# A fused delta-rule attention and ternary FFN on one core: half of the chunk inverses on GpSimd during the projection, the first two solve rounds in row halves

## The chip, the cores and the metric

The kernel runs on one core of a Trainium2 chip. The metric is the device time of one execution in microseconds. TensorE is PE here, VectorE DVE, ScalarE ACT, GpSimd POOL, and SyncE SP; SP and ACT issue the transfers.

## The reference

The input is x, 4 sequences of 2048 tokens with 256 channels, 4 heads of 64. In float32:

```
q, k, v = silu(conv4(x Wq)), silu(conv4(x Wk)), silu(conv4(x Wv));  beta = sigmoid(x Wb)
q, k normalised;  v = v * beta;  kb = k * beta
per head and chunk of 32 tokens:
    A = -(kb k^T) below the diagonal;  T = (I - A)^-1;  u = T v;  w = T kb
    attn = causal(q k^T);  u' = u - w S;  o = q S + attn u';  S = S + k^T u'
o = p0 fir3(v) + p1 fir15(v) + p2 fir63(v) + p3 o + p4 v     (p: softmax of gates, floored)
x = layernorm(x + rmsnorm(o) Wo)
x = layernorm(x + w3(gelu(h2(gelu(h1(silu(w1 x) * w2 x))))))
```

## The kernel before

It is four blocks with a barrier between them, each with hand-written queues per engine. Tokens go in 16 steps of 128 tokens of all 4 sequences, so a step holds 16 streams (4 sequences x 4 heads), `NS`.

**`project`.** For a step, PE makes six blocks (`cb` 0 to 5: two each of q, k and v) of projections (L224), ACT and DVE convolve them in `acc` (L334, L379), and ACT applies silu into `yT` (L307). Work of the step before is laid in between: `keys` turns k to tokens (`ktok`, L314) and forms the products k k^T of all 16 streams in `side`, copied to `kfull` (L324); `small` makes gates and the sums of q squared from `sq` (POOL, L424); `values` turns v to `vtok` (L395). The squared norm of k is the diagonal of k k^T: POOL picks it (`picked`, L434, four operations of 32 partitions), DVE sums it (`kk`, L398), and then POOL zeroes the 32x32 diagonal blocks and all left of them in `kfull` (L439). SP stores four pieces of the diagonal blocks as `a_s` (L176), and the rest as `kk_s` (L184), and loads `xt` of the step after next (L161). Twice in the block and once after it, `blocks_in` reads the diagonal blocks back into `tri`, whose partition is step and stream and whose 8 slots are 4 chunks x 2 groups of eight steps (L103).

**`weights_fir`.** DVE makes the mixing weights and the scales; `gamT` and `neg_gamT` are beta over the norm of k. Then come 64 rounds `n`. In a round PE convolves 4 channels with Toeplitz matrices (`conv`, L613), DVE multiplies with the weights (`prods`, L725), and POOL adds three parts in two operations (`two` L783, `mixed` L787). In rounds 0 to 59 DVE also does one operation of the forward substitution that inverts all 8 slots of `tri` in place: for column j an outer product (`outer`, L743) in an even round and the `update` (L747) in the odd one, 8j(31-j) elements each. The rows are scaled in two goes (L750), ACT turns the inverses (`turned_inv`, L641), and SP stores both as `d_s` and `t_s` (L566). SP loads the Toeplitz matrices in three pieces of 256-byte rows for each pair of rounds (L555), and the windows `win` of the next head (L548), the last of them when the head before has had its last round but two.

**`delta`.** The inverse of a 128-token block is built from the four 32x32 inverses by rounds of products: N = L x diag, A = N x diag^T, B and C repeated products, with partial copies by ACT (`nmat`, `r1`, `r2`, L1161) and sums by DVE in `tt` (L1244, L1246, L1261). They are made for step t+1 during step t. PE's order in a step is: state product, N, T (transposes), Q (q k^T), solve (L1063), W (output projection), outputs, A, B, C. ACT's is: N, T, the two `us`, `osq` once DVE has added `mix` to `o` (L1194), then A and B. DVE's is: Q, W, outputs, the sum over `osq` (L1290), statistics, terms A and B, C, then the right side and the norm. `N` needs banks that DVE's evacuation of the last C has freed.

**`ffn`** runs on PE with weights in two halves.

## Time and profile before

| | |
|---|---|
| three runs | 2434.59, 2437.59, 2437.62 us, median 2437.59 |
| the profiled execution | 2435.2 us, its span 2433.3 us |
| share of the span | PE 89%, DVE 51%, ACT 37%, POOL 24% |
| mean granted clock of TensorE | 0.956 |
| projection, weights and FIR, delta, FFN | 360.5, 251.8, 486.2, 1334.8 us |

The share of PE is a mean over four stages with different limits, and the chain that ended last, followed back, lies in the FFN alone. So the first three stages have to be read by their timelines. A row of a timeline has start, length, engine, line, operation and tiles, and in brackets how long the engine had been idle and what ended that. A float32 product is two records of PE.

### The profile page before, as it was taken

How to read it: one execution, taken by the hardware profiler on the slowest of the kernel's cores; microseconds unless marked ns; L12 is line 12 of the kernel's file. 1: busy time of each engine (PE TensorE's matmuls, PEld its weight loads, DVE VectorE, ACT ScalarE, POOL GpSimd, SP SyncE). 2: the span in 40 equal slices, each digit the busy share in tenths (PEclk: the TensorE clock that was granted, in tenths of full speed). 3: DMA queues.
4: the chain of work that ended last, by engine and by line, in shares of the span. 5: the costliest groups of instructions: out<-in, count | busy, mean ns of one | idle time of the engine just before them, and what ended most of it. 6: DMA issues, size and time to landing. Idle time of an engine off the chain costs nothing.

```text
span 2433.3 us, 40589 instructions
## 1 busy us (share of the span) xinstructions
PE 2157.0 (89%) x15412; PEld 1855.9 (76%) x15412; DVE 1235.5 (51%) x1872; ACT 895.2 (37%) x1425; POOL 593.4 (24%) x416
## 2 busy tenths in 40 slices
PE   7887865655699999967999999999999999999998
PEld 6776754555588888855888888888888888888887
DVE  5776758896477777762323332333333333323332
ACT  4554530002233334313434443444344334433442
POOL 2555555896344444430000000000000000000000
PEclk9999987887799999987999999999999999999999
DMA  3558759787989989925000000000000000000000
GB/s 131 194 197 204 194 200 211 198 207 236 241 229 249 250 235 241 254 79 219 1 18 17 0 17 17 17 0 17 17 17 0 17 17 17 0 17 17 18 1 18
DMA packets 346603, 257.53 MB, mean 106 GB/s; under 512 B 281394, under 2 KB 315698, under 8 KB 336434
## 3 DMA queue, kind: packets, MB, share of 16 engines
q1 hardware_dynamic: 333682, 232.65, 35.1%
q10 hardware_dynamic: 12864, 24.12, 2.8%
q8 instruction: 36, 0.59, 0.1%
q14 instruction: 21, 0.17, 0.0%
HBM read 156.85 MB, written 99.88 MB: 106 GB/s over the span
## 4 chain that ended last, share of the span: by engine, by line
PE 52%; issue 1%; DVE 1%; ACT 0%; DMA 0%; SPq 0%; POOL 0%; DVEq 0%; ACTq 0%; POOLq 0%
PE B L1611 46%; PE O L1639 5%; PE T L1567 1%; DVE yb L1738 0%; ACT gate L1677 0%; DMA wr<-wr_s 0%; SPq L1500 0%; DVE stats L1769 0%; ACT L1677 0%; DVE z L1764 0%; DVE z L1760 0%; DVE z L1783 0%; POOL rstd L1819 0%; SPq L1514 0%; DVEq L1733 0%
## 5 line engine op out<-in xcount | busy, mean ns | idle before, releaser
L1611 PE MATMUL B<-act1l,wr 128*128 128x512 f32 x1024 | 398.4, 389 | 0.0
L1611 PE MATMUL B<-act1h,wr 128*128 128x512 f32 x1024 | 398.3, 389 | 0.0
L1611 PE MATMUL B<-act0h,wr 128*128 128x512 f32 x1024 | 398.3, 389 | 0.0
L1611 PE MATMUL B<-act0l,wr 128*128 128x512 f32 x1024 | 398.3, 389 | 0.0
L1691 ACT ACTIVATE yb<-B,scol 128x512 f32<-128x512 f32 x256 | 176.2, 688 | 581.0 <-PE B L1611 581.0
L1726 DVE TENSOR_TENSOR act0l<-yb,act0h 128x512 fp32r<-128x512 f32 x256 | 176.1, 688 | 377.9 <-ACT act0h L1694 375.7
L1816 POOL TENSOR_TENSOR rstd<-mv,ln_eps 128x4 f32<-128x4 f32 x16 | 3.2, 199 | 1309.2 <-DVE mv L1777 1309.2
L379 DVE SCALAR_TENSOR_TENSOR acc<-proj,taps,acc 128x512 f32<-128x512 f32 x288 | 214.4, 750 | 92.3 <-ACT acc L334 83.7
L1726 DVE TENSOR_TENSOR act1l<-yb,act1h 128x512 fp32r<-128x512 f32 x128 | 88.6, 692 | 295.5 <-ACT act1h L1694 295.5
L224 PE MATMUL proj<-xt,w_qkv 128*128 128x262 f32 x768 | 195.0, 400 | 35.9 <-DMA xt<-in_xt 19.4
L1611 PEld LDWEIGHTS B<-act1h,wr 128*128 128x128 f32 x1024 | 192.2, 188 | 39.9
L1611 PEld LDWEIGHTS B<-act0h,wr 128*128 128x128 f32 x1024 | 192.2, 188 | 39.9
L1611 PEld LDWEIGHTS B<-act0l,wr 128*128 128x128 f32 x1024 | 192.2, 188 | 39.9
L1611 PEld LDWEIGHTS B<-act1l,wr 128*128 128x128 f32 x1024 | 192.2, 188 | 39.9
L1611 PE MATMUL B<-xh,wr 128*128 128x512 f32 x512 | 202.7, 396 | 11.8 <-DMA wr<-wr_s 7.6
L613 PE MATMUL conv<-toe,win 128*128 128x192 f32 x512 | 139.2, 433 | 83.1 <-DMA win<-v_s 41.8
L1611 PE MATMUL B<-xl,wr 128*128 128x512 f32 x512 | 200.8, 392 | 0.0
L613 PEld LDWEIGHTS conv<-toe,win 128*128 128x128 f32 x512 | 127.8, 316 | 94.4 <-DMA win<-v_s 43.0
L224 PEld LDWEIGHTS proj<-xt,w_qkv 128*128 128x128 f32 x768 | 141.5, 192 | 72.2 <-DVE acc L379 28.6
L1738 DVE SCALAR_TENSOR_TENSOR yb<-B,scol,gate 128x512 f32<-128x512 f32 x128 | 94.8, 750 | 183.7 <-ACT gate L1677 128.1
L783 POOL TENSOR_TENSOR two<-prods 128x256 f32<-128x256 f32 x64 | 123.6, 1932 | 17.7 <-DVE prods L725 17.7
L1611 PEld LDWEIGHTS B<-xh,wr 128*128 128x128 f32 x512 | 97.0, 189 | 37.7 <-DVE yb L1738 10.1
(164 smaller groups left out, 3477.6 us busy)
## 6 DMA issues: line engine op xcount, KB each, us to landing
qk_s<-yT SPq DMA_DIRECT2D x16, 1024.0 KB, 5.8
kk_s<-kfull SPq DMA_DIRECT2D x16, 1024.0 KB, 3.9
qk<-qk_s SPq DMA_DIRECT2D x16, 1024.0 KB, 6.7
lt<-kk_s SPq DMA_DIRECT2D x15, 1024.0 KB, 5.3
wraw<-in_ffn_w ACTq DMA_DIRECT2D x16, 704.0 KB, 6.4
wr_s<-wround ACTq DMA_DIRECT2D x16, 704.0 KB, 9.5
toe<-in_firp SPq DMA_DIRECT2D x64, 160.0 KB, 3.6
xt<-in_xt SPq DMA_DIRECT2D x16, 524.0 KB, 4.0
```

What stands on the lines that cost most here:

```text
L224: last = nc.tensor.matmul(proj[cb % 2][:, 2 * half:2 * half + 2, 0:XW], w_qkv[:, k, cb * P:cb * P + P], xt[p][:, k, 2 * half:2 * half + 2, ...
L379: nc.vector.scalar_tensor_tensor(out=acc[cb % 3][:, :, :], in0=proj[cb % 2][:, :, j:j + P], scalar=taps[:, cb, j:j + 1], in1=acc[cb % 3][: ...
L613: last = nc.tensor.matmul(conv[n % 2][:, c // 2, c % 2 * NF * WIN:(c % 2 + 1) * NF * WIN], win[h % 2][:, :, g * FCH + c], toe[part % 2][:, ...
L783: nc.gpsimd.tensor_tensor(two[n % 2][:, :, :], part[:, 0, :, :], part[:, 1, :, :], ALU.add).then_inc(two_done, 1)
L1567: last = nc.tensor.transpose(T[:, k, b * P:b * P + P], x1[p][:, b, k * P:k * P + P], ident)
L1611: last = nc.tensor.matmul(B[slot % 4][:, :], w, part, start=(k == 0 and i == 0), stop=(k == kts - 1 and i == len(parts) - 1))
L1639: last = nc.tensor.matmul(O[:, b, :], sets[0][i][:, k, b * P:b * P + P], wr[:, W3 + k * D:W3 + k * D + D], start=(k == 0 and i == 0), stop ...
L1691: last = nc.scalar.activation(dst, B[slot % 4][:, :], ACT.Gelu, scale=scol[:, slot:slot + 1])
L1726: nc.vector.tensor_tensor(sets[s][1][:, m, :], yb[n % 3][:, :], sets[s][0][:, m, :].bitcast(f32), ALU.subtract).then_inc(lo_done, 1)
L1738: nc.vector.scalar_tensor_tensor(out=dst, in0=B[(2 * m + 1) % 4][:, :], scalar=scol[:, HT + m:HT + m + 1], in1=gate[m % 2][:, :], op0=ALU. ...
L1816: nc.gpsimd.tensor_tensor(rstd[:, :], mv[:, :, 1:2].rearrange("p b o -> p (b o)"), ln_eps[:, :], ALU.add).then_inc(rs_link, 1)
```

## The change

In the projection, the norms of k come from `ktok` squared by POOL (`sqk`) and summed by DVE, so that `picked`, the mask, and `a_s` go; `kfull` is stored whole, and each step reads its own diagonal blocks back into `tri`. After step 8 the scales of the first eight steps are made, and POOL runs the substitution of their 4 slots, columns 1 to 24, between the squares of steps 10 to 16; the rest of the columns and the row scaling come first on POOL in the next block. There DVE does the other 4 slots, both operations of a column in one round, in rounds 0 to 29. The Toeplitz matrices come ready from DRAM in one transfer (0.79 MB) per pair of rounds. `d_s` and `t_s` are stored by halves at the pairs 2, 4, 18 and 20. In the delta stage, N and A are made in two products per stream, of 64 output rows each, over the columns that are filled; ACT copies the filled blocks in three (N) or two (A) pieces; and ACT's copies of A stand ahead of `osq`. The loops of the projection are partly written out. The diff, cut to its core:

```diff
-BLOCK_PARTS = ((0, STEPS // 2), (STEPS // 2, 3 * STEPS // 4), (3 * STEPS // 4, STEPS))
+NSUB = GRP // P
+EARLY_STEPS = STEPS // NSUB
+EARLY_COLS = {10: (1, 5), 11: (5, 9), 12: (9, 12), 13: (12, 15), 14: (15, 18), 15: (18, 21), 16: (21, 25)}
+EARLY_END = 25
...
-def blocks_in(queue, io, keep, part):
-    first, end = BLOCK_PARTS[part]
-    g, rows = first // (STEPS // 2), slice(first * NS % P, (end * NS - 1) % P + 1)
+def blocks_in(queue, io, keep, t):
+    first = t * NS % P
     for q in range(NQ):
-        queue.dma_start(keep["tri"][rows, q * (GRP // P) + g, :, :],
-                        io["a_s"][q * CH:q * CH + CH, first * NS:end * NS, :].rearrange("i n j -> n i j")
-                        ).then_inc(keep["tri_in"], 16)
+        queue.dma_start(keep["tri"][first:first + NS, q * NSUB + t // EARLY_STEPS, :, :],
+                        io["kk_s"][q * CH:q * CH + CH, t * NS:t * NS + NS, q * CH:q * CH + CH].rearrange("i n j -> n i j")
+                        ).then_inc(keep["tri_in"][t // EARLY_STEPS], 16)
...
+class Substitution:
+    def __init__(self, engine, keep, half, outer):
+        self.engine, self.slots = engine, slice(half, SLOTS, NSUB)
+        self.tri, self.outer = keep["tri"][:, self.slots, :, :], outer
+        self.gamT, self.neg_gamT = keep["gamT"][:, self.slots, :], keep["neg_gamT"][:, self.slots, :]
+    def scaled_columns(self):
+        for r in range(0, CH, 8):
+            g = self.neg_gamT[:, :, 0:r + 8]
+            g = bass.AP(tensor=g.tensor, offset=g.offset, ap=[g.ap[0], g.ap[1], [0, 8], g.ap[2]])
+            last = self.engine.tensor_tensor(self.tri[:, :, r:r + 8, 0:r + 8], self.tri[:, :, r:r + 8, 0:r + 8], g, ALU.mult)
+        return last
+    def products(self, j):
+        return self.outer[:, 0:SLOTS // NSUB * (CH - 1 - j) * j].rearrange("p (s i c) -> p s i c", s=SLOTS // NSUB, c=j)
+    def outer_product(self, j):
+        row = self.tri[:, :, j, 0:j]
+        row = bass.AP(tensor=row.tensor, offset=row.offset, ap=[row.ap[0], row.ap[1], [0, CH - 1 - j], row.ap[2]])
+        return self.engine.tensor_tensor(self.products(j), bcast(self.tri[:, :, j + 1:CH, j], j), row, ALU.mult)
+    def update(self, j):
+        below = self.tri[:, :, j + 1:CH, 0:j]
+        return self.engine.tensor_tensor(below, below, self.products(j), ALU.add)
+    def scaled_rows(self):
+        return self.engine.tensor_tensor(self.tri, self.tri, bcast(self.gamT, CH), ALU.mult)
+    def zero_above(self):
+        for i in range(CH - 1):
+            last = self.engine.memset(self.tri[:, :, i, i + 1:CH], 0.0)
+        return last
+    def ones_on_diagonal(self):
+        return self.engine.memset(self.tri.rearrange("p s i j -> p s (i j)")[:, :, 0:CH * CH:CH + 1], 1.0)
...
-                    for q in range(NQ):
-                        rows = slice(q * CH, q * CH + CH)
-                        sp.dma_start(io["a_s"][rows, bass.ds(t * NS, NS), :], kfull[p][rows, :, rows]).then_inc(diag_stored[p], 16)
+                    sp.dma_start(io["kk_s"][:, t * NS:t * NS + NS, :], kfull[p][:, :, :]).then_inc(kk_stored[p], 16)
                     sp.wait_ge(ktok_out, n)
                     sp.dma_start(row(io["k_s"], t), ktok[p][:, :, :]).then_inc(k_stored[p], 16)
                     sp.wait_ge(vtok_out, n + 1)
-                    sp.dma_start(io["v_s"][:, :, bass.ds(t + 1, 1), :, :].rearrange("h p o b d -> p h (o b d)"),
+                    sp.dma_start(io["v_s"][:, :, t + 1:t + 2, :, :].rearrange("h p o b d -> p h (o b d)"),
                                  vtok[p][:, :, :, :].rearrange("p h b d -> p h (b d)")).then_inc(v_stored[p], 16)
-                    sp.wait_ge(kk_masked, n)
-                    sp.dma_start(io["kk_s"][:, bass.ds(t * NS, NS), :], kfull[p][:, :, :]).then_inc(kk_stored[p], 16)
+                    sp.wait_ge(kk_stored[p], 16 * (t // 2 + 2))
+                    blocks_in(sp, io, keep, t)
...
+                    early = isinstance(t, int) and t == EARLY_STEPS + 1
+                    if early:
+                        pe.wait_ge(gam0_done, 1)
+                        nc.tensor.transpose(gam_ps, gam0[:, :, :, :].rearrange("p t r s -> p (t r s)"), ident).then_inc(gam0_turned, 1)
                     turn(lambda hh, b: yT[p][:, KT + hh, b * P:b * P + P]).then_inc(ktok_ready, 1)
+                    if early:
+                        pe.wait_ge(gam0_out, 2)
...
+                    if isinstance(t, int) and t == EARLY_STEPS + 1:
+                        act.wait_ge(gam0_turned, 1)
+                        for scale, dst in ((-1.0, keep["neg_gamT"]), (1.0, keep["gamT"])):
+                            nc.scalar.activation(dst[:, 0:SLOTS:NSUB, :], gam_ps.rearrange("p (q i) -> p q i", i=CH),
+                                                 ACT.Copy, scale=scale).then_inc(gam0_out, 1)
...
+                    act.wait_ge(sqk_done, t + 1)
                     nc.scalar.activation(ktok[p][:, :, :], tok[:, :, :], ACT.Copy).then_inc(ktok_out, 1)
                     act.wait_ge(kk_stored[p], n * 16 + 16)
-                    act.wait_ge(kk_summed, t + 1)
...
+                nc.scalar.activation(ebeta[:, :, :], raw[:, 0:NE, NGATE:NGATE + HEADS], ACT.Exp, scale=-1.0).then_inc(exp0_done, 1)
...
-                    dve.wait_ge(diag_picked, t * NQ + NQ)
                     nc.vector.tensor_copy(vtok[p][:, :, :, :].rearrange("p h b d -> p b h d"),
                                           tok[:, :, :].rearrange("p b (h d) -> p b h d", d=DK)).then_inc(vtok_out, 1)
-                    nc.vector.tensor_reduce(kk[:, bass.ds(t, 1), :, :].rearrange("p o r s -> p (o r s)"), picked[p][:, :, :],
-                                            AX.X, ALU.add).then_inc(kk_summed, 1)
+                    dve.wait_ge(sqk_done, t + 3)
+                    nc.vector.tensor_reduce(kk[:, bass.ds(t, 1), :].rearrange("p o h -> p (o h)"),
+                                            sqk[:, :, :].rearrange("p b (h d) -> p (b h) d", d=DK), AX.X, ALU.add).then_inc(kk_summed, 1)
+                def first_scales():
+                    def link(ins, n):
+                        ins.then_inc(gam0_link, 1)
+                        dve.wait_ge(gam0_link, n)
+                    dve.wait_ge(kk_summed, EARLY_STEPS + 2)
+                    nc.vector.tensor_scalar(ssk0[:, :, :].rearrange("p (t b) h -> p t (b h)", b=BATCH), kk[:, 0:EARLY_STEPS, :],
+                                            L2_EPS, None, ALU.add)
+                    dve.wait_ge(exp0_done, 1)
+                    link(nc.vector.tensor_scalar(ebeta[:, :, :], ebeta[:, :, :], 1.0, None, ALU.add), 1)
+                    link(nc.vector.tensor_tensor(half0[:, :, :], ssk0[:, :, :], ebeta[:, :, :], ALU.mult), 2)
+                    link(nc.vector.reciprocal(half0[:, :, :], half0[:, :, :]), 3)
+                    for par in range(2):
+                        last = nc.vector.tensor_copy(gam0[:, :, par, :],
+                                                     half0[:, :, :].rearrange("p (t b) (k r) -> p t r (b k)", t=EARLY_STEPS, r=2)[:, :, par, :])
+                    last.then_inc(gam0_done, 1)
...
-                def diagonals(t, p, n):
-                    for q in range(NQ):
-                        rows = slice(q * CH, q * CH + CH)
-                        if q:
-                            pool.wait_ge(diag_picked, t * NQ + q)
-                        nc.gpsimd.tensor_tensor(picked[p][rows, :, :], kfull[p][rows, :, rows],
-                                                bcast_mid(const[rows, C_ONE:C_ONE + CH], NS), ALU.mult).then_inc(diag_picked, 1)
-                    pool.wait_ge(diag_stored[p], n * (16 * NQ) + 16 * NQ)
-                    pool.wait_ge(diag_picked, t * NQ + NQ)
-                    nc.gpsimd.tensor_tensor(kfull[p][:, :, :], kfull[p][:, :, :], bcast_mid(const[:, C_OFF:C_OFF + P], NS),
-                                            ALU.mult).then_inc(kk_masked, 1)
...
+                def key_squares(t, p):
+                    pool.wait_ge(ktok_out, t + 1)
+                    pool.wait_ge(kk_summed, t + 2)
+                    nc.gpsimd.tensor_tensor(sqk[:, :, :], ktok[p][:, :, :], ktok[p][:, :, :], ALU.mult).then_inc(sqk_done, 1)
...
+                for t in range(STEPS + 1):
+                    if t < STEPS:
+                        squares(t, t % 2)
+                    if t:
+                        key_squares(t - 1, 1 - t % 2)
+                    if t == EARLY_STEPS + 1:
+                        pool.wait_ge(keep["tri_in"][0], 16 * NQ * EARLY_STEPS)
+                        sub.zero_above().then_inc(keep["sub_link"], 1)
+                    if t in EARLY_COLS:
+                        first, end = EARLY_COLS[t]
+                        if first == 1:
+                            pool.wait_ge(gam0_out, 2)
+                            pool.wait_ge(keep["sub_link"], 1)
+                            sub.scaled_columns().then_inc(keep["sub_link"], 1)
+                            pool.wait_ge(keep["sub_link"], 2)
+                            sub.ones_on_diagonal()
+                        early_columns(nc, pool, sub, keep, first, end)
+def early_columns(nc, pool, sub, keep, first, end):
+    for j in range(first, end):
+        pool.wait_ge(keep["sub_link"], 2 * j)
+        sub.outer_product(j).then_inc(keep["sub_link"], 1)
+        pool.wait_ge(keep["sub_link"], 2 * j + 1)
+        sub.update(j).then_inc(keep["sub_link"], 1)
...
-                    for f, k in enumerate(FIRS):
-                        src = io["firp"]
-                        sp.dma_start(toe[n % 2][FIRST[f]:, :, f, :],
-                                     bass.AP(tensor=src.tensor, offset=(n * TCH * NF + f) * FIRPAD + FIRST[f],
-                                             ap=[[1, P - FIRST[f]], [NF * FIRPAD, TCH], [1, WIN]])).then_inc(toe_in[n % 2], 16)
+                    sp.dma_start(toe[n % 2][:, :, :, :], io["toe"][n]).then_inc(toe_in[n % 2], 16)
...
+                    if n in D_OUT:
+                        sp.wait_ge(inv_done[D_OUT[n]], 1)
+                        blocks_out("d_s", tri, D_OUT[n])
+                    if n in T_OUT:
+                        sp.wait_ge(turned[T_OUT[n]], 1)
+                        blocks_out("t_s", turned_inv, T_OUT[n])
...
-                    j = n // 2 + 1
-                    if j <= COLS:
-                        link(outer_product(j) if n % 2 == 0 else update(j))
-                    if n + 1 == ROWS_EARLY or n + 1 == 2 * COLS:
-                        if n + 1 == ROWS_EARLY:
-                            dve.wait_ge(upper_zero, 1)
-                        rows = slice(0, EARLY) if n + 1 == ROWS_EARLY else slice(EARLY, CH)
-                        scaled_rows(rows).then_inc(inv_done, 1)
+                    if n < COLS:
+                        link(sub.outer_product(n + 1))
+                        link(sub.update(n + 1))
+                    if n == COLS:
+                        dve.wait_ge(upper_zero, 1)
+                        sub.scaled_rows().then_inc(inv_done[1], 1)
...
+                late = Substitution(nc.gpsimd, keep, 1, None)
+                pool.wait_ge(tri_in[1], 16 * NQ * EARLY_STEPS)
+                late.zero_above().then_inc(above_zero, 1)
+                sub = Substitution(nc.gpsimd, keep, 0, keep["outer0"])
+                early_columns(nc, pool, sub, keep, EARLY_END, CH - 1)
+                pool.wait_ge(keep["sub_link"], 2 * (CH - 1))
+                sub.scaled_rows().then_inc(inv_done[0], 1)
                 pool.wait_ge(columns_scaled, 1)
-                for i in range(CH - 1):
-                    nc.gpsimd.memset(tri[:, :, i, i + 1:CH], 0.0)
-                last = nc.gpsimd.memset(tri[:, :, :, :].rearrange("p s i j -> p s (i j)")[:, :, 0:CH * CH:CH + 1], 1.0)
-                last.then_inc(upper_zero, 1)
+                late.ones_on_diagonal().then_inc(upper_zero, 1)
...
+        FILLED = {"N": ((slice(0, P // 2), slice(0, CH)), (slice(P // 2, P), slice(0, 3 * CH))),
+                  "A": ((slice(0, P // 2), slice(CH, P)), (slice(P // 2, P), slice(3 * CH, P)))}
...
-                        elif kind in "NABC":
+                        elif kind in "NA":
+                            for j in range(4):
+                                c = par * BH + half * 4 + j
+                                for out, cols in FILLED[kind]:
+                                    left = (lt if kind == "N" else nmat)[:, c, out]
+                                    right = (ddiag[p] if kind == "N" else tdiag[p])[:, c, cols]
+                                    last = nc.tensor.matmul(bank[out, j, cols], left, right, start=True, stop=True)
+                        elif kind in "BC":
...
-                        rows, cols = REGION.get(kind, (slice(0, P), slice(0, P - CH if kind == "N" else P)))
-                        if kind == "T":
-                            dst = oT[:, g, :].rearrange("p (b n) -> p b n", b=BATCH)
-                        else:
-                            dst = {"N": nmat, "A": r1, "B": r2}[kind][rows, c, cols]
+                        if kind == "N":
+                            for rows, cols in BELOW:
+                                last = nc.scalar.activation(nmat[rows, c, cols], bank[rows, :, cols], ACT.Copy)
+                            last.then_inc(act_out, 1)
+                            continue
+                        if kind == "A":
+                            for rows, cols in ABOVE:
+                                last = nc.scalar.activation(r1[rows, c, cols], bank[rows, :, cols], ACT.Copy)
+                            last.then_inc(act_out, 1)
+                            continue
+                        rows, cols = REGION.get(kind, (slice(0, P), slice(0, P)))
+                        dst = oT[:, g, :].rearrange("p (b n) -> p b n", b=BATCH) if kind == "T" else r2[rows, c, cols]
...
+                    if pre:
+                        copy_rounds("A", seq, round0)
                     act.wait_ge(mixed, t + 1)
                     nc.scalar.activation(osq[:, :, :, :], o[:, :, :, :], ACT.Square).then_inc(sq_done, 1)
                     if pre:
-                        copy_rounds("A", seq, round0)
```

## Rows read from the trace of the kernel before

**Rows 1.** Busy time by stage: stretch, length, engines, PEclk, DMA share, GB/s
```profile
0.00:360.50 360.50, 291.72 (x2560) 236.73 (x2560) 246.24 (x352) 168.56 (x275) 184.75 (x101) 0.96 0.63 188
360.50:612.30 251.80, 141.47 (x562) 129.61 (x562) 201.66 (x151) 21.96 (x14) 184.01 (x163) 0.78 0.81 213
612.30:1098.50 486.20, 418.11 (x6018) 391.06 (x6018) 333.53 (x617) 168.44 (x321) 205.21 (x119) 0.95 0.85 221
```

**Rows 2.** Waits of the projection: us in total, times, longest
```profile
PE proj L224 <- DMA xt<-in_xt: 19.4, 3, 9.0
```

**Rows 3.** Timeline of SP's queue in the projection
```profile
191.66 13.07 SPq L103 DMA_DIRECT2D tri<-a_s  x4
```

**Rows 4.** Timeline of ACT in the projection, the copies of `ktok`
```profile
191.69 1.01 ACT L314 ACTIVATE ktok<-tok 128x1024 f32<-128x1024 f32 x1
...
219.41 1.02 ACT L314 ACTIVATE ktok<-tok 128x1024 f32<-128x1024 f32 x1 [0.28 <-PE tok L233]
...
340.82 1.02 ACT L314 ACTIVATE ktok<-tok 128x1024 f32<-128x1024 f32 x1 [0.23 <-ACT yT L307]
```

**Rows 5.** Timeline of DVE in the projection
```profile
316.90 0.68 DVE L398 TENSOR_REDUCE kk<-picked 128x512 f32 x1
```

**Rows 6.** Groups by form in the projection: busy us, mean ns, idle before
```profile
L439 POOL TENSOR_TENSOR kfull<-kfull,const 128x2048 f32<-128x2048 f32 x16 | 72.6, 4535 | 14.2 <-DMA a_s<-kfull 12.9
...
L424 POOL TENSOR_TENSOR sq<-yT 128x1024 f32<-128x1024 f32 x16 | 30.3, 1893 | 145.7 <-PE side L273 128.1 <-ACT yT L307 17.7
```

**Rows 7.** Groups by line, 362 to 600 us
```profile
L783 POOL TENSOR_TENSOR two<-prods 128x256 f32<-128x256 f32 x64 | 123.6, 1932 | 17.7 <-DVE prods L725 17.7
...
L747 DVE TENSOR_TENSOR tri<-tri,outer 128x240 f32<-128x240 f32 (+14 forms) x30 | 56.2, 1872 | 0.0
```

**Rows 8.** Timeline of the rounds
```profile
395.15 0.96 DVE L725 TENSOR_TENSOR prods<-conv,pwT 128x768 f32<-128x768 f32 x1 [1.96 <-ACT pwT L659]
...
486.40 0.96 DVE L725 TENSOR_TENSOR prods<-conv,pwT 128x768 f32<-128x768 f32 x1
...
494.28 6.70 PE L613 MATMUL conv<-toe,win 128*128 128x192 f32 x24 [8.13 <-DMA win<-v_s]
...
561.14 8.62 PE L613 MATMUL conv<-toe,win 128*128 128x192 f32 x32 [1.38 <-DMA toe<-in_firp]
...
583.48 0.40 DVE L743 TENSOR_TENSOR outer<-tri 128x240 f32<-128x240 f32 x1
```

**Rows 9.** The stage's end: timeline, and the busy times of ten us
```profile
596.37 0.73 POOL L787 TENSOR_TENSOR mixed<-two,prods 128x256 f32<-128x256 f32 x1
...
598.27 1.46 SPq L562 DMA_DIRECT2D mix_s<-mixed  x1
...
600.00:610.00 10.00, 0.00 (x0) 0.00 (x0) 0.00 (x0) 0.00 (x0) 0.00 (x0) 0.50 1.02 423
```

**Rows 10.** Timeline of one step of the delta stage
```profile
826.64 2.96 PE L1032 MATMUL R<-tdiag,nmat 128*96 128x96 f32 x32
...
829.45 1.06 ACT L1194 ACTIVATE osq<-o 128x1024 f32<-128x1024 f32 x1 [9.67 <-DVE o L1286]
...
830.41 3.08 ACT L1161 ACTIVATE r<-R 96x384 f32<-96x384 f32 x8
830.54 1.22 DVE L1290 TENSOR_REDUCE ss<-osq 128x16 f32<-128x1024 f32 x1 [1.12 <-ACT osq L1194]
...
831.02 3.18 PE L1032 MATMUL R<-r,nmat 128*64 128x64 f32 x64 [1.43 <-ACT r L1161]
...
836.62 3.81 PE L1032 MATMUL R<-ddiag,lt 128*128 128x96 f32 x32 [0.36 <-DVE tt L1261]
```

**Rows 11.** The same stage: timeline of two solves; group by form of ACT's copies
```profile
815.90 2.08 PE L1063 MATMUL Y<-x,tt 128*64 128x64 f32 x64
...
843.22 2.08 PE L1063 MATMUL Y<-x,tt 128*64 128x64 f32 x64
...
L1161 ACT ACTIVATE nmat<-R 128x384 f32<-128x384 f32 x52 | 25.5, 491 | 56.4 <-PE R L1032 56.4
```

191 lines of the change are left out of this document (78 added, 113 removed).

## The prediction

> **What bounds the kernel now.** I read the busy times by stage first [rows 1]. The program is four blocks in a row: projection (0 to 360.5 us), weights and FIR (to 612.3), delta rule (to 1098.5), FFN. The FFN is not touched, so only the first three can move; the chain that ended last starts inside the FFN and says nothing of them. For those I went through the timelines and asked which wait closes each loop.
>
> *Projection.* No engine is full. One step takes 20.2 us (six from 219.4 to 340.8 [rows 4]), and DVE's convolution of block 5, ACT's copies and PE's products close a circle. The exception is one step: `tri<-a_s` holds SP's queue 13.07 us [rows 3], so the next `xt` is late (three waits of PE for `xt`, the first load's among them, make 19.4 us [rows 2]), and 27.7 us lie between two `ktok` copies instead of 20.2: 7.5 us lost.
>
> *Weights and FIR.* In 64 rounds PE convolves, DVE weighs and does one substitution product, GpSimd adds twice. DVE and GpSimd take turns: `two` averages 1.93 us [rows 7], and the addition of the same size without DVE beside it 0.73 [rows 9]. At each new head PE stops for `win` (8.13 us) [rows 8].
>
> *Delta.* A step is 27.3 us, from solve to solve [rows 11]. PE is busy through most of it, but what lets the next step begin is DVE: it idles until ACT's `osq` is done, then works without a gap for 6.1 us, and round N starts behind the evacuation of round C [rows 10].
>
> **The change, part by part.** Each is a difference against the profiled 2435.2 us (span 2433.3), 2.4 us under the median 2437.6, which I carry over unchanged.
>
> *Projection, removed.* The bulk reads of `a_s` become four 64 KB reads per step, as many issues as the `a_s` stores that go; SP's wait for `kk_stored` ends before `vtok` is stored, hence free. The lost 7.5 us return: **-7.5**. If the four small reads hold SP like the large ones, this is 0.
>
> *Projection, DVE.* The sum over `picked` (512 elements, 0.68 us [rows 5]) becomes one over `sqk` (1024 elements). The delta stage's sum of that shape takes 1.22 us [rows 10]. The wait for `picked` that goes is about 0.25. On the circle, +0.3 in some 14 steps: **+4.2**. `first_scales` waits once for ACT's Exp, with a table load there and one back, and does six small operations on DVE; `keys` of step 9 waits for one transpose and two copies; no row prices them, I take **+3.7** together (0 to 8).
>
> *Projection, GpSimd.* `picked` and the mask (4.5 us a step) leave, `key_squares` comes (1.9, as `sq` [rows 6]). Of the substitution, column j has two operations of 4j(31-j) elements. At 2.2 ns an element (2048 in 4.54 us [rows 6]) the fullest step, columns 21 to 24 (6080 elements), costs 13.4 us, the other full ones 11 to 12.6. With 3.8 us of squares, 16.4 lie under the 20.2 of a step, so PE's wait for `sq` stays covered; at over 2.8 ns an element it would not be. Behind the last `ktok` copy (341.8 [rows 4]) GpSimd needs 1.9 + 13.4 us: 357 to 358. SP's last store, `kk_s` behind the mask, goes out with the copies of `kfull` and no longer ends the block: **-2.2** (to +2).
>
> *Second stage, start.* Loop start now 34.6 us behind the stage's (395.15 [rows 8]). The late read of `tri`, the `toe` memsets and two thirds of the Toeplitz issues go. But GpSimd first does 31 memsets (4 us), columns 25 to 30 (4480 elements, 9.9) and the scaled rows (4096 elements, 9.0), taking turns with DVE's softmax work. I put the start at 32: **-2.5** (-8 to +4).
>
> *Rounds 0 to 29.* Half the slots, but both operations of a column in one round: by round 30 DVE has multiplied and added 39,680 elements, exactly what it has done by then today, in 60 operations instead of 30. An operation of 240 elements takes 0.40 us [rows 8], 30 of them with 39,680 elements 56.2 us [rows 7], which is 1.04 ns an element and 0.5 each, of which about 0.15 is its own and 0.35 GpSimd's turn. Thirty more cost 4 to 15; I take 8. The head's stall at round 16 (8 us for PE, some 6 for DVE, which has rounds in hand) falls under DVE's longer rounds, the two early 2 MB stores (`d_s`, `t_s`) delay a Toeplitz load by some 3: **+5** (-1 to +15).
>
> *Rounds 30 to 63.* Today 110.7 us (486.40 [rows 8] to 597.1 [rows 9]), with DVE's operation in nearly all. After it: scaled rows 4.4, then only the weighing (0.96) and GpSimd's two additions (1.5) against PE's 2.15 a round (8.62 for four [rows 8]): 33 rounds are 71 us. Per two rounds the queues move 0.79 MB of `toe` and, for one head, 0.52 of `win`, with `mix_s` 1.57 MB; at 263 GB/s (213 at a share of 0.81 [rows 1]) that is 6.0 us, at the 423 of the stretch with only large stores [rows 9] 3.7, against PE's 4.3; large rows prevail, so I lean to the second, and the late stores 4 MB more: 8 us of waiting. Two head changes, one half hidden: 8. Sum 91.5: **-19** (-32 to -5).
>
> *Its end.* The last `mix_s` store (issued at 598.3 [rows 9], the stage ending at 612.3) stands behind 4 MB of `t_s` and more of `d_s` and takes 12 us to land; alone, about 5: **-6.5**. Stage: **-23**.
>
> *Delta, round N.* Per slot one product of 128x128 by 96 columns (119 ns a record [rows 10]) becomes two with 64 rows, 32 and 96 columns wide, each two records. Round pairs on alternating halves take 32.5 ns a record (2.08/64 [rows 11]); B and C, not alternating, average 50 [rows 10]. So halves overlap, and the 96-column half sets the time, at round A's 92 ns: 16x2x92 = 2.9 us instead of 3.8. ACT now copies in three pieces (128, 256 and 128 elements; 0.49 us for 384 [rows 11] and 1.06 for 1024 [rows 10] make 0.26 and 0.38, pipelined about 0.79) instead of 0.49, so it paces the round, and Q waits for its banks. Gain 0.3 a step (from 0.4 to a loss of 0.3).
>
> The Trainium skill ("TensorE: Matmul & The Clock Gate", section "The mechanism") says that a weight load overlaps running matmuls only when the row group differs, which it does not here. By that N and A would each be some 4.2 us. The alternating records above speak against it.
>
> *Delta, round A.* It already has 96 columns, so its 2.96 us stay. ACT's copies now come before `osq`: the last A bank is ready 3.15 us after A's start, its two copies end at 3.8, `osq` at 4.9. Today `osq` ends at 3.9 [rows 10]. PE's 1.43 us wait for the first copy of A goes, but PE isn't what closes the step: DVE's sum waits for `osq`, and behind it stand statistics, both terms, C's evacuation and so N. Loss 1.0 a step (0.65 to 1.75). Net +0.7 in 14 steps: **+10**.
>
> Sum: -1.8 - 23 + 10 = **-15 us**, 2437.6 - 15 = 2423.
>
> **The rivals.** *Forecast, with its own range 2408 to 2433:* chance 0.50.
>
> *Halves do not overlap* (slower). The two products of a slot run one after the other: (40 + 92)x2x16 ns = 4.2 us for N and A, 40 being what is left for C's records in the 3.18 us that B and C take. A's last copy then ends near 5.1, `osq` at 6.1, 2.2 late, and N loses 0.4: +2.6 a step, +36. With -23 and -2 from the other stages, 2449. It decides from about 1.8 us a step. For it: such unequal halves aren't in the trace. Against: rows 11. Chance 0.12.
>
> *GpSimd's turns cost more* (no change, or slower). If a column's second operation waits for a whole addition and the start waits for the 9 us scaled rows, rounds 0 to 29 cost +15 and the start +4; with the transfers nearer 263 GB/s in the second half the stage gains only 10. 2437.6 - 2 - 10 + 10 = 2436, up to 2443. For it: `two` at 1.93. Chance 0.20.
>
> *The second half runs at PE's pace, the delta stage is even.* No queue waits in rounds 31 to 63, SP's stall gone, the copies packed: 2437.6 - 35 - 4 + 3 = 2402. For it: the single contiguous `toe` transfer in place of three of 256-byte rows. Against: `win` still arrives late at each head. Chance 0.16.
>
> *The early inverses don't hide.* GpSimd above 2.8 ns an element, each step 10 to 16 drawn out by 2 to 3 us: +15, near 2438. Against: 2.2 is measured beside the same DVE work. Chance 0.02.
>
> **How the numbers follow.** This kernel's runs tell 0.2%, 4.9 us, from no change. The forecast's range lies mostly beyond it: 0.46 faster, 0.04 same; the fast case 0.16 faster; the costly turns 0.04 faster, 0.08 same, 0.08 slower; no overlap 0.12 slower; the last 0.02 same. So 0.66 faster, 0.14 same, 0.20 slower. The range of 8 in 10 runs from inside the fast case to between the two slow ones: 2400 to 2446.
>
> **What the profile would show.** Right: no wait of PE for `xt` but the first; `ktok` copies about 20.5 us apart; GpSimd's 960-element operations near 2.1 us, `sq` never awaited; in the second stage rounds of 3.1 us, then of 2.2; delta steps of 28.0 us with DVE's wait for `osq` near 2.1 instead of 1.1; N near 2.9. Wrong: N at or over 3.8 and A over 3.5 (no overlap); rounds above 2.6 us after the thirtieth (transfers); a delta step under 27.3, which would mean DVE's stretch does not close the circle and the 0.7 has the wrong sign.

## The result and the profile after

| | us, median | runs | ratio to before, 95% interval |
|---|---|---|---|
| before | 2436.1 | 2431.0 to 2437.6 | |
| after | 2483.9 | 2479.5 to 2486.9 | 1.0199 (1.0176 to 1.0221) |

The change makes the kernel 2.0% slower, some 48 us. Forecast was 2423. The profiled execution has a span of 2485.1 us, against 2433.3 before.

The busy times by stage of the kernel after, in the columns of [rows 1]:

```profile
0.00:359.90 359.90, 293.65 (x2561) 237.78 (x2561) 255.40 (x358) 171.62 (x279) 146.22 (x121) 0.97 0.61 179
359.90:598.20 238.30, 139.16 (x561) 129.91 (x561) 158.11 (x149) 21.13 (x12) 151.78 (x174) 0.79 0.74 247
598.20:1149.00 550.80, 431.02 (x7042) 399.74 (x7042) 347.51 (x618) 217.74 (x513) 192.41 (x119) 0.89 0.72 197
```

The first stage is even (359.9 instead of 360.5), the second 13.5 us shorter, and the third 64.6 us longer. In the third, TensorE's granted clock has fallen from 0.95 to 0.89 and PE has 1024 more records, yet only 13 us more busy time. So it waits. Who for, by the waits of PE there (us in total, times, longest):

```profile
PE R L1071 <- DMA tdiag<-t_s: 47.3, 8, 15.6
PE X L1101 <- issue: 30.5, 6, 5.3
PE R L1082 <- ACT r L1219: 12.5, 15, 0.8
PE R L1057 <- ACT nmat L1209: 8.8, 12, 0.9
```

The second row is new. "issue" is time in which PE waited for nothing that the profile shows, and it stands ahead of X, the products from the state that open a step, 4.7 to 5.3 us in every second step: at each of the six branches back of PE's loop, which makes seven turns of two steps. The first row, PE's wait for `tdiag`, is longer than before too: there it is 36.5 us in three waits, here 3.4 to 4.3 us of it stand in six of the steps without a stop. PE's timeline around one of the stops, to be held against [rows 10]:

```profile
...
835.68 2.81 PE L1071 MATMUL R<-tdiag,nmat 128*64 128x96 f32 x64
838.32 2.16 PE L1082 MATMUL R<-r,nmat 128*64 128x64 f32 x32
841.32 1.22 PE L1082 MATMUL R<-r,nmat 128*32 128x32 f32 x32 [0.83 <-ACT r L1219]
847.86 3.75 PE L1101 MATMUL X<-S,qk 128*128 128x128 f32 x16 [5.32 <-issue]
851.54 3.85 PE L1071 MATMUL R<-ddiag,lt 128*64 128x32 f32 x64
...
```

After the stop, X takes 3.75 us instead of 2.05, and N 3.85 instead of 2.86: the granted clock was 0.54 over the 5 us of the stop and 0.50 over the next 3.5 us, the 1.2 GHz level. The page's list of DMA queues (packets, MB, share) says what else has grown; before it was 36 packets and 0.59 MB:

```profile
q8 instruction: 97, 1.59, 0.3%
```

What was forecast of the third stage is there too. In a turn's good step (start at 805.68) `osq` comes 4.03 us behind A instead of 2.81, DVE's sum waits for it 2.24 us instead of 1.12, and ACT copies N's slots in threes, of which PE's Q waits 0.9 for the last:

```profile
805.68 2.81 PE L1071 MATMUL R<-tdiag,nmat 128*64 128x96 f32 x64
...
809.71 1.06 ACT L1254 ACTIVATE osq<-o 128x1024 f32<-128x1024 f32 x1
...
810.80 1.22 DVE L1351 TENSOR_REDUCE ss<-osq 128x16 f32<-128x1024 f32 x1 [2.24 <-ACT osq L1254]
...
818.04 2.86 PE L1071 MATMUL R<-ddiag,lt 128*64 128x32 f32 x64 [3.48 <-DMA tdiag<-t_s]
...
822.84 2.27 PE L1057 MATMUL R<-qk 64*128 64x128 f32 x32 [0.92 <-ACT nmat L1209]
```

A step here is 30.0 us, against 27.3 before [rows 11], and 34.2 with the stop in it; over eleven steps the mean is 32.5.

The second stage, from the waits of PE after its rounds have begun, and PE and SP where the longest one falls:

```profile
PE conv L678 <- DMA toe<-in_toe: 30.1, 12, 8.2
PE conv L678 <- DMA win<-v_s: 22.9, 3, 8.5
```
```profile
514.72 8.81 PE L678 MATMUL conv<-toe,win 128*128 128x192 f32 x32 [1.36 <-DMA toe<-in_toe]
531.75 8.63 PE L678 MATMUL conv<-toe,win 128*128 128x192 f32 x32 [8.22 <-DMA toe<-in_toe]
```
```profile
515.54 0.60 SPq L636 DMA_DIRECT2D d_s<-tri  x1
...
519.59 0.33 SPq L627 DMA_DIRECT2D toe<-in_toe  x1
...
524.44 0.59 SPq L636 DMA_DIRECT2D t_s<-turned_inv  x1
536.89 0.33 SPq L627 DMA_DIRECT2D toe<-in_toe  x1
```

### The profile page after: what moved, and what is told of

Same layout as the page of the kernel before. It is cut to its first block, busy times and chain, and to the rows that moved or that the text cites. A ratio compares the mean times of both kernels' runs of the same rounds, so it can differ in the third digit from the quotient of the medians.

```text
span 2485.1 us, 42333 instructions
## 1 busy us (share of the span) xinstructions
PE 2169.3 (87%) x16436; PEld 1865.8 (75%) x16436; DVE 1215.1 (49%) x1877; ACT 946.8 (38%) x1620; POOL 509.8 (21%) x447
## 3 DMA queue, kind: packets, MB, share of 16 engines
q8 instruction: 97, 1.59, 0.3%
## 4 chain that ended last, share of the span: by engine, by line
PE 51%; issue 1%; DVE 1%; ACT 0%; DMA 0%; SPq 0%; POOL 0%; DVEq 0%; ACTq 0%; POOLq 0%
PE B L1672 45%; PE O L1700 5%; PE T L1628 1%; DVE yb L1799 0%; ACT gate L1738 0%; DMA wr<-wr_s 0%; SPq L1561 0%; DVE stats L1830 0%; ACT L1738 0%; DVE z L1825 0%; DVE z L1821 0%; DVE z L1844 0%; POOL rstd L1880 0%; SPq L1575 0%; DVEq L1794 0%
## 5 line engine op out<-in xcount | busy, mean ns | idle before, releaser
L259 PE MATMUL proj<-xt,w_qkv 128*128 128x262 f32 x768 | 196.6, 403 | 29.3 <-DVE acc L439 20.2
L678 PE MATMUL conv<-toe,win 128*128 128x192 f32 x512 | 137.1, 432 | 80.1 <-DMA win<-v_s 32.5
L1209 ACT ACTIVATE nmat<-R 32x128 f32<-32x128 f32 (+1 forms) x192 | 58.6, 305 | 228.4 <-PE R L1071 226.1
```

The source lines that it names most:

```text
L259: last = nc.tensor.matmul(proj[cb % 2][:, 2 * half:2 * half + 2, 0:XW], w_qkv[:, k, cb * P:cb * P + P], xt[p][:, k, 2 * half:2 * half + 2, ...
L678: last = nc.tensor.matmul(conv[n % 2][:, c // 2, c % 2 * NF * WIN:(c % 2 + 1) * NF * WIN], win[h % 2][:, :, g * FCH + c], toe[part % 2][:, ...
L1209: last = nc.scalar.activation(nmat[rows, c, cols], bank[rows, :, cols], ACT.Copy)
```

## The experiments

All figures are medians, with the interval of the ratio to the kernel before, timed beside it on the same chip. The kernel before itself had medians of 2434.1 to 2437.3 there, so a difference between kernels that were timed on different chips is good to some 3 us. A step's length is the mean over eleven steps, from SP's loads of `lt`.

### Which stage

**e1_delta_of_before**: the function `delta` of the kernel before in the kernel after. `kk_s` comes unmasked there, and this `delta` does not clear what lies above the diagonal, so the mask is left out of the computation. 

> The kernel after the change, but the third stage (delta) is the one of the kernel before, with its 384-element copies, full-width products of rounds N and A and osq ahead of the A copies. The trace of after puts the loss in the third stage (550.8 us instead of 486.2) and a gain of 14 us in the first two. If that reading holds (theory T), this kernel takes 2436 - 14 = 2422, range 2416 to 2428, and its third stage 486 +- 4. Rival: part of the loss is carried over from the first two stages (later stores of the inverses, another layout of the program), then it stays above 2440.

Measured 2421.0, 0.9937 (0.9920 to 0.9954), a step 27.33. **e2_only_delta**: the function `delta` of the kernel after in the kernel before. 

> The kernel before, with the third stage (delta) of the kernel after alone. Theory T (the stages add up): 2436 + 62 = 2498, range 2490 to 2506, with waits of PE called issue ahead of the products from the state (X) in every second step and the queue 8 of instructions at some 95 packets. Rival: the third stage of after only loses because its inverses or buffers come in another way from the new stages, then 2436 to 2450.

Measured 2478.5, 1.0165 (1.0146 to 1.0184), a step 30.67, 65 packets in queue 8. So the first two stages give 16 us and the third takes it back four times over. It takes 63 us with the new stages ahead of it (2483.9 less 2421.0) but only 41 with the old ones, which I had not expected: something in `delta` depends on what stands ahead of it. One difference is in the trace. Of the six branches back, in e2 only every second one has a stop (5.3 to 5.9 us); the other three have 0.2 us.

```profile
729.88 2.02 PE L1064 MATMUL X<-S,qk 128*128 128x128 f32 x16 [0.22 <-issue]
...
793.74 3.76 PE L1064 MATMUL X<-S,qk 128*128 128x128 f32 x16 [5.62 <-issue]
```

### Which part of the third stage

**e3_full_products** and **e4_unrolled** start from the kernel after:

```diff
e3:
-for out, cols in FILLED[kind]:
-    left = (lt if kind == "N" else nmat)[:, c, out]
+rows_out, cols_out = (slice(0, P), slice(0, P - CH)) if kind == "N" else REGION["A"]
+left = (lt if kind == "N" else nmat)[:, c, rows_out]
e4:
-with pe.Fori(0, MID // 2) as i:
+for i in range(MID // 2):
```

> The kernel after; rounds N and A of the third stage are made again by one product of full width for each slot (16 fewer instructions a round), while ScalarE keeps its copies by filled blocks and its order (A copies ahead of osq). Theory 1 (the longer loop of TensorE is what costs: its instructions are fetched again in every turn): queue 8 back to some 36 packets, no waits called issue ahead of X, granted clock of the third stage back to 0.94, time 2422 + 10 = 2432, range 2424 to 2442. Theory 2 (ScalarE's order and its three copies cost): the loss stays, 2465 to 2485, with the waits called issue gone or not.

> The kernel after, with TensorE's loop over the steps of the third stage written out, so that no branch goes back; the products and waits are the same. Theory 1 as a miss at the branch back: more packets in queue 8 than after's 97 (about 120), but the waits of 5.3 us ahead of X are gone or under 1 us, time 2440 to 2455. Theory 1 as a bandwidth of fetching: as after or worse, 2475 to 2500, with waits called issue spread over other lines. Theory 2 (ScalarE's order and copies): 2475 to 2485 with the waits gone.

Measured 2466.1, 1.0121 (1.0104 to 1.0138), and 2461.7, 1.0107 (1.0090 to 1.0124). Each takes away the stop ahead of X (0.2 to 0.4 us are left of it in e3, nothing in e4), and each only about 20 of the 63 us: e4 lies above the 2440 to 2455 that theory 1 gave it. Theory 1 alone falls. With full products and 41 packets a step is still 30.87: 3.5 us over e1's, and this is ScalarE's share.

**e5_order_alone** and **e6_copies_alone** put ScalarE's two edits singly into the kernel before, **e7_products_alone** the halving:

```diff
e5  +copy_rounds("A", seq, round0)
     act.wait_ge(mixed, t + 1); osq
e5  -copy_rounds("A", seq, round0)
e6  +N copied by BELOW (three pieces a group), A by ABOVE (two)
e7  +N: rows 0:64 and 64:128 over columns 0:96;  A: rows 0:64 and 64:96 over columns 32:128
```

> The kernel before, with one part of the third stage alone: ScalarE's copies of round A stand ahead of osq. The run with full products showed the next round N starting 11.3 us after round A instead of 10.0, because tt comes later. Order theory: 1.3 us a step over 14 steps, 2437 + 18 = 2455, range 2449 to 2461. Rival (ScalarE's pieces do all of it, the order alone is harmless because B's products no longer wait 1.4 for r): 2437 +- 5.

> The kernel before, with one part of the third stage alone: ScalarE copies round N's slots in three pieces and round A's in two (nmat is cleared once). Copies theory: one group of N takes 0.95 us instead of 0.49, so Q starts about 1.8 us later behind N: 14 x 1.9 = 27, 2437 + 27 = 2464, range 2452 to 2472. Rival (the order does it all, copies lie beside the products): 2437 +- 5.

> The kernel before, with one part of the third stage alone: rounds N and A are made in row halves, over all the columns that the old copies read, so twice the instructions of TensorE for the same elements. Fetching theory (the loop of two steps no longer stays loaded): queue 8 at some 65 packets or more, a wait called issue in every turn, 2437 + 20 = 2457, range 2445 to 2465. Rival 1 (the halves overlap and take back a part, no fetching): 2437 - 10 to 2437. Rival 2 (halves do not overlap): 14 x 5.8 = 2437 + 80.

Measured 2458.9, 1.0104 (1.0082 to 1.0126); 2460.2, 1.0106 (1.0089 to 1.0123); 2521.2, 1.0344 (1.0302 to 1.0386). Order and pieces cost 22 and 24 us, and together, e3 less e1, 45: they add up. In e5 N waits 2.1 to 2.5 us for `tt` in every step (0.36 before [rows 10]), and sometimes that costs a second time: of thirteen such rounds two took 6.8 us, five 5.4 and the others 3.8. N's row and the window over it (PE, PEld, DVE, ACT, POOL busy, clock, DMA share, GB/s), with the clock at 0.53, for an N of 6.81 us instead of 3.81:

```profile
815.98 6.81 PE L1032 MATMUL R<-ddiag,lt 128*128 128x96 f32 x32 [2.51 <-DVE tt L1275]
```
```profile
816.00:822.70 6.70, 6.70 (x33) 6.70 (x34) 4.14 (x10) 1.47 (x3) 1.90 (x2) 0.53 1.07 357
```

In e6 the pieces act at two places, N and, unforeseen, A. Eight copies of 64 rows and fewer take 3.11 us where four of 96x384 took half that, B's copies and with them C come later, and B and C take 4.14 us instead of 3.18 [rows 10]:

```profile
810.03 3.11 ACT L1175 ACTIVATE r<-R 64x384 f32<-64x384 f32 x8
...
810.92 4.14 PE L1043 MATMUL R<-r,nmat 128*64 128x64 f32 x64 [1.71 <-ACT r L1175]
```

e7 is no clean test of the halving, since I cut A into 64 and 32 rows: A took 9.49 us instead of 2.96, while N, in 64 and 64 rows, took 2.86 instead of 3.81.

```profile
810.83 2.86 PE L1034 MATMUL R<-ddiag,lt 128*64 128x96 f32 x64
...
827.27 9.49 PE L1034 MATMUL R<-tdiag,nmat 128*64 128x96 f32 x64
```

These two do not add up to its 85 us. Its undisturbed step is 31.2 us instead of 27.3, which is 3.9 for the 6.5 and -0.95, and four of its branches back have the stop:

```profile
PE X L1064 <- issue: 28.2, 4, 7.9
```

A step with the stop is some 8.7 us longer: 14 x 3.9 + 4 x 8.7 = 89, 85 measured. So a good third of e7 is the stops too, with 74 packets in queue 8.

**e8_order_undone**: the kernel after with the old order. 

> The kernel after, with osq ahead of the A copies again, as before. Order theory: 2484 - 18 = 2466, range 2458 to 2474. Rival (order harmless): 2484 +- 5.

Measured 2501.2, 1.0271 (1.0254 to 1.0289). A miss of the other sign: 17 us slower than after. Its undisturbed step is 29.7 us, 0.3 shorter, but its stops ahead of X are longer, 7.7 to 8.7 us instead of 4.7 to 5.3. What the order costs alone it does not cost beside the stops; why the stop grows was not tried.

**e9_pieces_for_N** keeps of the new `delta` only N's pieces; **e10_half_N_added** adds N's row halves to it:

```diff
e9, in delta of the kernel after, with the products of e3 and the order of before:
-for rows, cols in ABOVE:
-    last = nc.scalar.activation(r1[rows, c, cols], bank[rows, :, cols], ACT.Copy)
+nc.scalar.activation(r1[rows, c, cols], bank[rows, :, cols], ACT.Copy)      (rows, cols of REGION["A"])
e10, for N alone:
+for out, cols in FILLED["N"]:
+    last = nc.tensor.matmul(bank[out, j, cols], lt[:, c, out], ddiag[p][:, c, cols], start=True, stop=True)
```

> The kernel after, its third stage changed back to full-width products in N and A, one copy of 384 elements a group for A, and osq ahead of the A copies; only N's copies stay in three pieces. If the parts add up, the pieces of N alone cost 0.4 to 0.6 us a step (Q starts 5.0 instead of 4.6 behind N, as in the run with the copies alone) and the pieces of A the rest of that run's 1.6: 2421 + 7 = 2428, range 2423 to 2434. Rival (N's pieces are the costly ones): 2440 or more.

> The kernel of the run before, with round N alone in row halves over its filled columns (16 more products a step, half of what the change adds). Fetching theory with a limit by length: queue 8 at 60 to 97 packets, a wait called issue of 3 to 6 us in every turn of the two-step loop, 2428 + 20 = 2448, range 2438 to 2460. If the loop of this length still stays loaded: 36 to 41 packets, no such wait, N 1 us shorter but Q still behind the copies: 2420 to 2428.

Measured 2428.5, 0.9975 (0.9964 to 0.9987), and 2480.0, 1.0186 (1.0169 to 1.0203). So N's pieces cost 7.5 us over e1 (9 by the ratios), and by difference A's pieces, which were not run alone, cost the other 16 of e6. And sixteen more products a step bring the whole of the stops back, for 51 us where I had said 20, although N itself is 0.9 us shorter:

```profile
809.95 2.05 PE L1108 MATMUL X<-S,qk 128*128 128x128 f32 x16
812.44 2.86 PE L1078 MATMUL R<-ddiag,lt 128*64 128x32 f32 x64 [0.44 <-DVE tt L1326]
...
834.59 3.18 PE L1089 MATMUL R<-r,nmat 128*64 128x64 f32 x64 [1.43 <-ACT r L1224]
844.09 3.75 PE L1108 MATMUL X<-S,qk 128*128 128x128 f32 x16 [6.32 <-issue]
```

### What the stops are

**e11_before_unrolled**, **e13_padded_by_16** and **e14_padded_by_8** are the kernel before with more code and its own work; **e16_half_N_unrolled** is e10 with the loop written out.

```diff
e13, e14, behind the waits of from_state:
+for _ in range(16):      (8 in e14)
+    nc.tensor.matmul(X[0][0:1, 0, 0, 0:1], qk[p][:, KT, 0:1], S[:, 0, 0, 0:1], start=True, stop=True)
```

> The kernel before, with TensorE's loop over the steps of the third stage written out: the same products and waits, only more code, each fetched once. Fetching theory: some 75 packets in queue 8 instead of 36, waits called issue of some 3 us a step as in the written-out kernel after, 2437 + 25 = 2462, range 2450 to 2485. Rival (fetching is free as long as no branch goes back, and the waits in the written-out kernel after came from its late inverses): 2437 +- 5.

> The kernel before, with 16 products of one element each added to every step of TensorE's loop, behind the waits of the products from the state (they write a bank that is overwritten next). The work stays that of before, the loop grows by as many instructions as half of round N's halves add. If the length of the loop alone brings the fetching: queue 8 near 92 packets, a wait called issue of some 6 us in every turn, 2437 + 50 = 2487, range 2465 to 2500. Rival (the fetching needs the denser rows of instructions of the halved rounds): 36 packets, 16 x 0.03 to 0.06 us a step, 2437 to 2450.

> As the run before with 8 such products a step. If the loop's limit lies between the loop of before (which stays loaded) and that plus 16: either 36 packets and 2437 to 2443, or near 92 packets and 2465 to 2500; nothing between, for the loop either stays or is fetched whole. I take the second, 0.6: the written-out loop took 3 packets of 16 KB a step, so two steps are 6, and partly filled ones at both ends make it 7 or 8.

> The kernel with pieces for N and halves in N alone, with TensorE's loop over the steps written out. If only the branch back costs: no wait called issue ahead of X, 2428 - 2 = 2426, range 2420 to 2432. If the halved round is too dense for the fetching (the written-out kernel after waited 3.5 us a step ahead of N): 2440 to 2460, with that wait again.

Measured 2438.2, 1.0009 (0.9999 to 1.0020), 72 packets; 2439.9, 1.0015 (1.0005 to 1.0024), 37 packets; 2449.0, 1.0051 (1.0035 to 1.0068), 91 packets; 2430.5, 0.9968 (0.9956 to 0.9979), 81 packets. Written out, the code is fetched in passing and costs nothing that can be told; so it is the branch back that costs. But length does not decide: with 16 products more nothing is fetched again, with 8 more something is. The step of e14 is 27.4 us all the same, and its time falls between the two cases of which I had said that nothing lies between. Its stops lie elsewhere, in the loop of the FFN, whose code nobody had touched:

```profile
PE B L1613 <- issue: 10.5, 6, 2.1
```

That pointed to where a loop lies. I counted TensorE's instructions of 64 bytes in the compiled programs, in blocks of 16 KB (a packet of queue 8 is 1.59 MB / 97 = 16 KB). The counts are in no profile:

```
            delta's loop        FFN's loop         packets   PE waits for issue
before      14.02 to 20.21  7   37.44 to 43.80  7     36     none
e13         14.27 to 20.96  7   38.44 to 44.80  7     37     none
e14         14.15 to 20.58  7   37.94 to 44.30  8     91     in FFN
e9          19.15 to 25.33  7   42.57 to 48.93  7     41     none
e10         19.65 to 26.33  8   43.57 to 49.93  7     96     in delta
after       20.15 to 27.33  8   44.57 to 50.93  7     97     in delta
e2          15.02 to 22.21  8   39.44 to 45.80  7     65     in delta
```

The number behind a stretch is how many blocks it touches; waits of 0.5 us and less are left out. The loops are 6.19 blocks long before, 6.69 with 16 products more a step, 7.19 with 32. The packets bear the lengths out: written out, the six further turns bring 36 packets more than before in e11 (6.0 a turn) and 40 more than e9 in e16 (6.7 a turn). Where a loop starts, only the count says. A shift of 0.1 block is in all of these; I chose it, and from 0.08 to 0.13 the table comes out as runs show: a loop that touches seven blocks stays loaded, one that touches eight is fetched again. e10, after and the FFN of e14 have six stops each, with 54 to 56 packets more than where the loop stays (e10 less e17, after less e9, e14 less before), some nine for each stop. e2 has three, and e7, whose loop has as many products as e2's, has four, with 29 and 38 packets more than before, nine or ten for each. Why it is nine and not eight, and why some turns are spared, no run shows. Of the program's two FFN loops it is the one of 6.36 blocks; that this one runs is argued from the packets of before, 36 of the program's 50.

The Trainium skill ("Runtime: NRT & Kernel Launch", section "Instruction fetch mechanics") says that PE's instruction memory holds 128 KiB and is refilled in blocks of 16 KiB, and that a taken branch whose target lies outside the current window of two blocks has to wait until the target is fetched. The runs agree in kind, with stops of 2 to 9 us. By the 128 KiB an estimate of the limit would be eight blocks, and the runs put it at seven; by the window of two blocks the loop of before would stall in each turn too, and no row shows that.

**e17_half_N_shifted** puts this to the test: e10, and nothing but 35 small products in the step ahead of the loop.

```diff
+if isinstance(t, int) and t == 0:
+    for _ in range(35):
+        nc.tensor.matmul(X[0][0:1, 0, 0, 0:1], qk[p][:, KT, 0:1], S[:, 0, 0, 0:1], start=True, stop=True)
```

> The kernel of the run half_N_added (2480 us, 96 packets), with 35 products of one element in the first step of the third stage, outside the loop: 140 instructions of 64 bytes that move the loop by 0.55 of a block of 16 KB. Counted in the compiled programs, that loop lay over 19.55 to 26.23 blocks and was fetched again; the padded loop of equal length at 14.17 to 20.86 was not. Placement theory (the loop stays loaded if it touches no more than 7 blocks): it now lies at 20.09 to 26.78, queue 8 back to 41 packets, no wait called issue, 2428, range 2422 to 2434. Rival (length or density of the halved round): still 96 packets, 2478 to 2484.

Measured 2422.9, 0.9954 (0.9937 to 0.9971): 57 us faster than e10 with more code and more work. This is one shift in one kernel; no other was tried. Queue 8, and the opening of two steps in a row:

```profile
q8 instruction: 42, 0.69, 0.1%
```
```profile
792.25 2.05 PE L1111 MATMUL X<-S,qk 128*128 128x128 f32 x16
...
820.08 2.02 PE L1111 MATMUL X<-S,qk 128*128 128x128 f32 x16
```

### The second stage, and the best version

**e12_late_inverse_stores**: e9 with `D_OUT, T_OUT = {2: 0, 25: 1}, {4: 0, 27: 1}`. 

> The kernel with pieces for N alone, with the second stores of the inverses (d_s and t_s, 2 MB each) moved from pairs 18 and 20 to pairs 25 and 27 of the second stage, into the last head, where no window is loaded. The trace of after shows PE waiting 8.2 us for toe behind these two stores. If they only collided with the windows there, the stage gains 5 us (range 2 to 8): 2423. Rival (the bytes are to be moved anyway; the wait moves with them): no difference, +-3 against that kernel, or slower by the end of the stage.

Measured 2428.8, 0.9973 (0.9960 to 0.9986): nothing. PE's waits for `toe` went from 29.5 to 27.1 us, and those for `win` from 20.9 to 24.8. The rival holds in so far as the wait moves with the stores; that the bytes set the pace is argued and not shown.

**e15_lower_blocks_loaded** keeps the old copies by leaving nothing above the diagonal to clear, **e18_best** adds N in full-width row halves and e17's shift.

```diff
e15 -load_kk(t + 2, lt, lt_in)
e15 +for q in range(NQ - 1):      (lt is cleared once)
e15 +    rows, cols = slice(q * CH, q * CH + CH), slice(q * CH + CH, P)
e15 +    sp.dma_start(lt[rows, :, cols], io["kk_s"][rows, bass.ds(t * NS, NS), cols]).then_inc(lt_in, 16)
e18 +N: rows 0:64 and 64:128 over columns 0:96;  35 small products ahead of the loop
```

> The kernel with pieces for N alone, changed so that only the blocks of kk_s above the diagonal of lt are loaded (three transfers of 384, 256 and 128 byte rows instead of one of 1 MB) into an lt cleared once; nmat then is zero above and is copied in one piece again. If the loads stay hidden, the step falls from 28.0 to 27.3 us: 2428 - 9 = 2419, range 2414 to 2425. Rival (1536 more small rows a step delay tdiag and ddiag, N waits for them): 2428 to 2450.

> The kernel with the lower blocks loaded (2420 us), with round N made in row halves over all 96 columns, in place of one product, and the same 35 small products ahead of the loop. If the loop stays loaded and N is on the path of the step: N 2.9 instead of 3.7 us, Q 0.8 earlier, 14 x 0.8 = 11, 2409, range 2404 to 2415. Rival (DVE's chain closes the step, N's gain is lost again): 2418 to 2424. If the loop is fetched again: 2460 or more.

Measured 2419.7, 0.9925 (0.9909 to 0.9942), and 2414.4, 0.9924 (0.9908 to 0.9941). Both beat both kernels: 0.75% under before. In e18's trace a step is 26.9 us, and 26.7 but for one long one, where e15 has 27.3. So of N's 0.8 us the trace shows 0.4 to 0.6 a step, but the ratios do not tell the two kernels apart, and the gain is not secured.

## Why the prediction was wrong, by its steps

- *Projection, removed (-7.5)*: right. PE waits for `xt` once, for the first load. *DVE's sum (+4.2)*: too dear. The last three intervals of `ktok` are 20.2 us on average, as in [rows 4], and the first seven 20.4 against 20.3, so most of it lies beside other work. *`first_scales` and `keys` (+3.7)*: three steps of 21.7, 22.7 and 23.1 us make +6.8, inside its bounds. *Its end (-2.2)*: not separately seen; the stage gains 0.6 where -1.8 was said.
- *GpSimd's early columns*: right, down to the price. The 960-element operations take 1.91 and 2.04 to 2.24 us, and PE never waits for `sq`.
- *Second stage, start (-2.5)*: right, 32.6 us. *Rounds 0 to 29 (+5)*: right, 97.0 us from `prods` of round 0 to that of round 30 instead of 91.3, +5.8. *Its end (-6.5)*: 4.4 us behind the last `mixed` instead of 15.2, -10.8. *Rounds 30 to 63 (-19)*: mis-sized, 104.2 us instead of 110.7, -6.5. I gave 8 us to the queues and 8 to the heads; PE waits there 19.8 us for `toe` and 14.7 for `win`. That leaned on 423 GB/s for large rows, and these rounds moved 255. The stage gives 13.5, not 23.
- *Delta, round N (gain 0.3 a step)*: its first half was right, 2.86 us where 2.9 was said, so the halves overlap and that rival is out. The pieces take 0.95 us a group, not 0.79, and by themselves cost 7.5 us (e9 against e1).
- *Delta, round A (loss 1.0)*: the mechanism was right, DVE waits 2.24 for `osq` where 2.1 was said. The size was short: 22 us alone, 1.6 a step, in e5, as N's 2.3 us of idleness is at times followed by N at half clock. And the sentence that A's copies "end at 3.8" counted their end but not that B's copies stand behind them: the pieces of A are 16 us, by the difference above, that are in no term.
- *The step that failed*, *net +0.7 in 14 steps: +10*, is the sum over all instructions by their durations; the delta stage took 63 us more (after less e1). The sum has no term for the number of instructions itself. I priced 32 more products a step at nothing but their time, and did not ask where they are kept. Of the 63 us, order and pieces are 45 (e3 less e1), where I had 14 for the order and a gain of 0.3 a step with N's pieces in it. The halved products are the other 18: a gain of a few us in N, and the stops, which alone are worth 57 (e10 less e17) where ScalarE does not hold PE up anyway.
- Every rival was inside the same frame. None of the five had a price beyond +36 in the delta stage, and the range ended at 2446.

What stays open: why a stop is 4.7 to 5.3 us in after, 5.3 to 7.6 in e10 and 7.7 to 8.7 in e8, why some turns of e2 and e7 have none, and how much of the 47.3 us for `tdiag` is the transfer's. In the step shown `tt` was done at 817.42, only 0.6 us before N started.

## What to carry over

Count the instructions of a loop on each engine, not only their time: here a loop that touched eight blocks of 16 KB instead of seven was fetched again at most of its branches back, and the stop of some microseconds took the clock down with it. The symptoms are a wait called issue at the top of a turn and queue 8 grown by whole loops, and the cheapest cure tried was moving the loop. When an engine paces a round, splitting its copies by what is filled saves elements and costs instructions, so price everything that is queued behind the last piece.

## What had not been expected of the hardware

- The place of a loop in memory decides: e10 and e17 have the same loop and differ by 57 us. Eight small products a step in the delta stage made the FFN wait, up to 2.1 us a turn and 10.5 in all, and the kernel slower by some 12 us (e14).
- Row halves of 64 and 64 overlap (32 products of 96 columns in 2.86 us, 45 ns a record), the row parts of 64 and 32 did not (9.49 us, 148 ns a record), in the same kernel (e7).
- After 2.5 us without work, TensorE at times came back at a granted clock of 0.53 and ran the next round in 6.81 instead of 3.81 us; after 5.3 us in the stops at 0.50.
- Whether `lt` comes as 1 MB in 128 long rows or as 0.4 MB in 1536 rows of 128 to 384 bytes made no difference to the step (e1, 27.33 us; e15, 27.32).
